# A decoder layer on one core: the last slice of the long convolutions moved from ahead of the delta stage into its first step

## The chip, the cores and the metric

The kernel runs on one core of a Trainium2 chip. The metric is device microseconds (us) from start to end of one execution, as the median of several; less is better. TensorE (PE) does matrix products, with its weight loads shown apart as PEld; VectorE (DVE) and ScalarE (ACT) do elementwise work; GpSimd (POOL) helps; SyncE (SP) issues nearly all DMAs, in the order of its own program.

## The reference

`x` and `ctx` are 8 x 256 x 256, float32. The part that the change touches is the first third:

```python
q, k, v = silu(dwconv(hs @ Wq, conv_q)), ...           # short convolutions, 4 taps
beta = sigmoid(hs @ Wb)
o_d = delta_rule_chunkwise(q, k, v, beta)              # per chunk: T = inv(I - attn); u = T @ v; w = T @ kb; scan over chunks
paths = stack([dwconv(v, fir_s), dwconv(v, fir_m), dwconv(v, fir_l), o_d, v])   # FIRs of 3, 15 and 64 taps
stats = [mean, mean square, mean abs, norm] of every path per head
probs = softmax(gelu([hs, stats] @ gW1 + gb1) @ gW2 + gb2, ...)
o = rmsnorm(sum_p probs_p * paths_p) @ Wo              # then x = layernorm(x + o)
```

Cross attention, a layer norm, and a mixture of 8 experts beside 2 shared ones follow; the change leaves them alone.

## The kernel before

Every engine has its own instruction stream, written out by Python generators; semaphores tie the streams together. `weave(stages, n, before, beside)` runs a software pipeline: in step s it interleaves, round by round (a round ends at each `yield`), stage k on batch s - k for all k, and after them the piece `beside[s]`.

**Projection phase** (`phase_project_invert_and_fir`). It ends with the long convolutions (`pe_fir`): they are products with Hankel matrices of the filters. There are 8 slices (`SLICES`) of 32 channels; slice `sl` reads the matrices in `env.hank[sl % 4]` (four buffers, loaded by SP) and the tokens in `win`. A slice has 4 pairs (`PAIRS`); a pair is 8 products of 128 x 32 weights with 192 columns (16 records in the trace, since each product is recorded twice), into one bank of PSUM: banks 0 to 3 for even slices, 4 to 7 for odd ones. ScalarE copies each pair out (`act_fir`, L685) to `stage[sl // 4]`, a half of the result. Semaphores: `fir_made` counts the pairs that TensorE has made (up to 32), `stage_copied` those that ScalarE has copied. `sp_stage(c)` (L613) writes half c to DRAM (`fir_dram`) in three DMAs of 1024 KB, when `stage_copied` has reached 16 or 32. In the same time VectorE inverts the diagonal blocks of all chunks, 128 of them in each of two groups: `dve_invert(0)`, then `dve_invert(1)` (L633, L636), whose last pieces run beside the delta stage.

**Delta stage** (`phase_delta_and_gate`, a pipeline over the 8 batches). Step s does the inverse of batch s (`pe_invert`, `act_invert`, `dve_invert`), the states of batch s - 1 (`pe_states` ...), the statistics of batch s - 2, the gate of batch s - 3, and the output product of batch s - 4. Rounds of `pe_invert`, which uses banks 0 to 3 only: 0 nothing; 1 turn k (L1053); 2 turn kb = k * beta (L1053; VectorE makes kb at L1167); 3 turn q (L1053); 4 the products kb x k (L1075, `a_made`); 5 the products k x q (L1084, `l_made`); 6 z1 (L1093), from ScalarE's copies at L1143 and L1145; 7 gw1 (L1102); 8 x1 and z2 (L1107, L1111); 9 gw2 (L1119). VectorE ends the step's inverse with L1189. The first instruction of step s + 1 on TensorE waits for that.

SP's order around the change, written out in `sp_first` and the weave: late Hankel matrices, first inverses out, tokens of batches 0 and 1 in (L1023), triangles of batch 0 (L1033, L1034), `sp_stage(0)`, triangles of batch 1, `sp_stage(1)`; then in step 1: the paths of batch 0 in (`sp_states(0)`, L1202 and L1204, which waits for all six writes of `fir_dram`), the tokens of batch 2 (L1023), its triangles, and so on. A DMA that waits holds up all that stand behind it on SP.

Ahead of the delta stage TensorE waits for all 32 pairs copied (`pe.wait_ge(fir.stage_copied, SLICES * PAIRS)`).

Of the kernel before, what the change touches and what calls it, by code (L numbers as in the profile page):

```python
# [15 lines left out]
B, T, D = 8, 256, 256  # L16
# [5 lines left out]
CH = 32  # L22
NCH = P // CH
TAPS = 4
FIRS = (3, 15, 64)
NF = len(FIRS)
# [3 lines left out]
BLK = 64  # L30
# [104 lines left out]
def weave(stages, n, before={}, beside={}):  # L135


    for s in range(n + len(stages) - 1):
        if s in before:
            before[s]()  # L140
        parts = [stage(s - k) for k, stage in enumerate(stages) if 0 <= s - k < n]
        interleave(parts + [beside[s]] if s in beside else parts)


def in_rounds(pieces, rounds):

    for r in range(max(rounds) + 1):
        if r in rounds:
            next(pieces, STOP)
        yield  # L150
# [11 lines left out]
def flat(t):  # L162
    return t.rearrange("p a b -> p (a b)")
# [59 lines left out]
SL = CH  # L223
# [3 lines left out]
HANK_DMAS = len(HANK)  # L227
NG = B * NP * NCH // P
PAIRS = SL // NCH // 2
SLICES = D // SL  # L230
RING = P // SL
# [10 lines left out]
def phase_project_invert_and_fir(pg, a, env):  # L242
    nc, pe, act, dve, pool, sp = pg.nc, pg.pe, pg.act, pg.dve, pg.pool, pg.sp
    V, S, G = nc.vector, nc.scalar, nc.gpsimd
    s = pg.signals("Project", "weights wpad_zero wpad raw_zero sel_zero sel_made filters_turned filters_copied filters_out xT_turned xT_copied raw_made raw_copied beta_made tanh beta first mac silu "
                   "sums_made sums_copied conv_turned sq v_copied ss rn_step tok kT_turned kT_copied a_made diag win_zero win_made fir_made stage_copied small_in tau_log eps_exp small",
                   "x_in rows_in sums_out tok_out diag_out am_in inv_set inv_step turned inv_out")
    with ExitStack() as mem:
# [5 lines left out]
        ps, ident = env.ps, env.ident  # L254
        win = top("win", [P, KT, B * NBLK, P])
# [13 lines left out]
        stage = [views(r, 0, n_stage, "p (f t c) -> p f t c", f=NF, t=BLK) for r in (room0, room1)]  # L269
# [378 lines left out]
        def pe_fir():  # L648
            yield
            yield  # L650
            pe.wait_ge(s.win_zero, 1)
            pe.wait_ge(s.win_made, B)
            pe.wait_ge(s.raw_copied, 3 * B)
            pe.wait_ge(s.sums_copied, B)
            for sl in range(SLICES):
                pe.wait_ge(env.hank_in[sl % RING], 16 * HANK_DMAS * (sl // RING + 1))
                for pair in range(PAIRS):
                    if sl >= 2:
                        pe.wait_ge(s.stage_copied, (sl - 2) * PAIRS + pair + 1)
                    elif sl == 0 and pair == 2:  # L660
                        pe.wait_ge(s.diag, NCH * B)
                    for u in range(2):
                        for q in range(NCH):
                            in_q = sl % RING * SL // NCH + pair * 2 + u
                            m = nc.tensor.matmul(ps[q * CH:(q + 1) * CH, sl % 2 * PAIRS + pair, u * NF * BLK:(u + 1) * NF * BLK],  # L665
                                                 win[:, sl // RING, :, q * CH + in_q],
                                                 env.hank[sl % RING][:, :, :, q * SL // NCH + pair * 2 + u].rearrange("k f s -> k (f s)"),
                                                 start=True, stop=True)
                    m.then_inc(*s.fir_made.up())
                    yield  # L670
                    if sl == 0 and pair == 1:
                        for _ in range(4):
                            yield

        def act_fir():
            for i in range(2):
                act.wait_ge(s.sums_out[i], 16 * B)
                act.wait_ge(s.tok_out[i], 16 * B // 2)
            exponentials = act_small()
            for sl in range(SLICES):  # L680
                next(exponentials, STOP)
                for pair in range(PAIRS):
                    c0 = sl % RING * SL // NCH + pair * 2
                    act.wait_ge(s.fir_made, sl * PAIRS + pair + 1)
                    S.copy(stage[sl // RING].rearrange("p f t c -> p c f t")[:, c0:c0 + 2, :, ::-1],  # L685
                           ps[:, sl % 2 * PAIRS + pair, 0:2 * NF * BLK].rearrange("p (c f t) -> p c f t", c=2, f=NF)
                           ).then_inc(*s.stage_copied.up())

# [57 lines left out]
        pool_win_zero()  # L748
        pool_hank_zero()
        weave([idle, idle, pool_normalise], B)  # L750
    env.sp_stage = sp_stage
    env.sp_inverses, env.sp_late_hank, env.sp_small, env.dve_small, env.projected = sp_inverses, sp_late_hank, sp_small, dve_small, s


# [109 lines left out]
def phase_delta_and_gate(pg, a, env):  # L864
    nc, pe, act, dve, pool, sp = pg.nc, pg.pe, pg.act, pg.dve, pg.pool, pg.sp
    V, S, G = nc.vector, nc.scalar, nc.gpsimd
# [7 lines left out]
    with ExitStack() as mem:  # L874
        def sb(n, shape, dt=F32):
            return mem.enter_context(nc.sbuf_tensor(n, shape, dt))
        ps, ident = env.ps, env.ident
# [21 lines left out]
        uT, u, oT = early("p (t c n) -> p t c n", n_x, 3, c=KT, t=TT)  # L899
# [28 lines left out]
        fir, FIR_OUT = env.projected, 16 * KT * NF  # L928
        GATE_IN, SMALL = 16 * 8, 8
        dve.wait_ge(fir.fir_made, (RING + 1) * PAIRS)  # L930
        pe.wait_ge(fir.stage_copied, SLICES * PAIRS)

        def pool_clear():
            pool.wait_ge(fir.fir_made, (RING + 1) * PAIRS)
# [64 lines left out]
        def dve_scale():  # L999
            dve.wait_ge(s.gate_in, GATE_IN)  # L1000
            V.tensor_scalar(flat(wo[:]), flat(wo[:]), nw[:, 0:1], None, ALU.mult).then_inc(*s.param.up())
            dve.wait_ge(fir.small, SMALL)

        def pe_await():
            pe.wait_ge(s.gate_in, GATE_IN)
# [157 lines left out]
        def dve_invert(b):  # L1163
            i, uses = b % 2, b // 2 + 1
            dve.wait_ge(s.tok_in[i], 16 * uses)
            dve.wait_ge(s.w_made, b - 1)
            V.tensor_tensor(heads(kb[i][:]), heads(tok[i][:, :, 1, :]), beta_of(b), ALU.mult).then_inc(*s.kb.up())  # L1167
            for _ in range(4):
                yield
            dve.wait_ge(s.u1_made, b - 1)  # L1170
            if b == 0:
                dve.wait_ge(fir.fir_made, SLICES * PAIRS)
            V.tensor_tensor(heads(vb[i][:]), heads(tok[i][:, :, 2, :]), beta_of(b), ALU.mult).then_inc(*s.vb.up())
            yield
            dve.wait_ge(s.l_made, b + 1)
            for h in range(HL):
                V.tensor_tensor(by_head(lT[i][:])[:, h], ps[:, 1 + h, :].rearrange("p (q j) -> p q j", j=P),
                                env.causal[:].unsqueeze(1).broadcast_to([P, NP // HL, P]), ALU.mult).then_inc(*s.lT.up())
            yield
            yield  # L1180
            dve.wait_ge(s.gw1_made, b + 1)
            for lo in LOW:
                V.tensor_copy(g0[i][lo:lo + CH, :, lo + CH:lo + 2 * CH],
                              ps[lo:lo + CH, 1, 0:NP * CH].rearrange("p (n j) -> p n j", j=CH)).then_inc(*s.gw.up())
            yield
            yield
            dve.wait_ge(s.gw2_made, b + 1)
            for h, bank in enumerate((3, 0)):
                V.tensor_copy(by_head(g0[i][:])[HS[0], h, :, HS[1]],  # L1189
                              ps[HS[0], bank, 0:NP // HL * DH].rearrange("p (q j) -> p q j", j=DH)).then_inc(*s.gw.up())  # L1190
            yield
# [560 lines left out]
        def rounds(of):  # L1752

            for r in range(max(of) + 1):
                for piece, b in of.get(r, ()):
                    piece(b)
                yield

        C, K, X, Q = pe_context, pe_keys_values, pe_turn_first, pe_first_query
        pe_beside = {9: rounds({3: ((C, 0), (C, 1)), 5: ((K, 0),)}),  # L1760
                     10: rounds({0: ((C, 2), (X, 0)), 1: ((K, 1),), 2: ((C, 3),), 3: ((C, 4),), 4: ((K, 2),), 5: ((K, 3), (C, 5))}),
                     11: rounds({0: ((K, 4),), 1: ((Q, 0),), 2: ((C, 6),), 3: ((K, 5), (C, 7)), 4: ((X, 1), (K, 6)), 5: ((Q, 1),), 6: ((K, 7),)})}
        C, K, X, Q = act_context, act_keys, act_turn_first, act_first_query
        act_beside = {9: rounds({3: ((C, 0), (C, 1)), 5: ((K, 0),)}),
                      10: rounds({0: ((C, 2), (X, 0)), 1: ((K, 1),), 2: ((C, 3),), 4: ((K, 2), (C, 4)), 5: ((K, 3), (C, 5))}),
                      11: rounds({0: ((K, 4),), 1: ((Q, 0),), 2: ((C, 6),), 3: ((K, 5), (C, 7)), 4: ((X, 1), (K, 6)), 5: ((Q, 1),), 6: ((K, 7),)})}
        v, Q = dve_values, dve_first_query
# [10 lines left out]
        sp_first()  # L1778
        weave([sp_invert, sp_states, sp_statistics, sp_gate, sp_project_out], B, {2: sp_rest, 3: sp_cross, 4: sp_filling},
              sp_beside)  # L1780
        weave([pe_invert, pe_states, idle, pe_gate, pe_project_out], B, {3: pe_await, 4: pe_await_scaled}, pe_beside)
        weave([act_invert, act_states, act_statistics, act_gate, act_project_out], B, {}, act_beside)
        weave([dve_invert, dve_states, dve_statistics, dve_gate, dve_project_out], B, {3: dve_scale}, dve_beside)
        pool_clear()
        weave([idle, idle, pool_statistics, pool_gate, pool_project_out], B,
              {9: lambda: pool_by_strip(pg, env, s.cross_in, s.pads, s.by_strip)})
# [1193 lines left out]
```

## Time and profile before

| | |
|---|---|
| median of 3 runs | 940.58 us (933.84, 940.95, 940.58) |
| the profiled execution: its own time | 944.34 us |
| its span, first to last instruction | 942.5 us |
| mean granted TensorE clock | 0.934 of full speed |
| busy share of the span: PE, PEld, DVE, ACT, POOL | 88%, 65%, 63%, 48%, 37% |
| L665, products of the long convolutions (512 records) | 44.2 us busy |

The clock has two levels in the trace, 1.00 (2.4 GHz) and 0.50 (1.2 GHz). Times in rows are us from the span's start. Line numbers of rows are those of the kernel before; in the order of the changed kernel the same lines stand 7 to 15 further down (L665 is L672, L685 is L693, L1053 is L1068).

### The profile page before, as it was taken

What the parts mean: (1) busy time and instruction counts of PE and PEld (TensorE: products, weight loads), DVE (VectorE), ACT (ScalarE), POOL (GpSimd) and SP (SyncE); (2) the same over time, 40 slices, a digit from 0 to 9 for tenths busy, and PEclk for the clock granted to TensorE, in tenths of its full rate; (3) what the DMA queues carried; (4) which work ended last, traced back from release to release, by engine and by line L of the source; (5) the groups of instructions that cost most, each with busy time, mean ns of one, the idle gap of its engine ahead of it and who ended that gap; (6) DMA issues with size and microseconds to landing.
All of it is one profiled execution on the core that took longest, in us unless ns stands there. A gap on an engine that the chain in (4) does not pass through costs nothing.

```text
span 942.5 us, 17146 instructions
## 1 busy us (share of the span) xinstructions
PE 826.7 (88%) x6187; PEld 615.5 (65%) x6187; DVE 592.9 (63%) x1431; ACT 448.9 (48%) x831; POOL 351.4 (37%) x321
## 2 busy tenths in 40 slices
PE   6888879779988988898578898899979999999895
PEld 5676657667766766677345555556866777777784
DVE  4799979664888888877546677763542333333256
ACT  5677747454656564453045665665412322322221
POOL 9421210011546555733202246335531342222684
PEclk9899979886999999799679999999998999999998
DMA  5679849987949875546644455308012222221411
GB/s 174 198 230 292 260 123 252 342 195 175 263 163 259 231 204 155 174 157 208 223 135 166 160 188 179 127 24 268 24 54 78 69 57 68 62 64 45 154 65 67
DMA packets 160722, 149.18 MB, mean 158 GB/s; under 512 B 92288, under 2 KB 129216, under 8 KB 159360
## 3 DMA queue, kind: packets, MB, share of 16 engines
q1 hardware_dynamic: 157232, 138.72, 50.1%
q0 software_dynamic: 3408, 9.38, 2.7%
q8 instruction: 51, 0.84, 0.4%
q14 instruction: 31, 0.25, 0.1%
HBM read 86.90 MB, written 61.03 MB: 157 GB/s over the span
## 4 chain that ended last, share of the span: by engine, by line
PE 54%; DVE 12%; ACT 12%; POOL 8%; DMA 6%; issue 5%; SPq 1%; POOLq 0%; DVEq 0%; ACTq 0%
PE ps L2730 10%; PE ps L2745 5%; PE ps L665 4%; PE ps L2594 3%; DMA queries<-q_pad 2%; DVE big L1449 2%; POOL hank L344 2%; POOL kept L2877 2%; PE ps L1397 2%; PE ps L2103 2%; PE ps L422 2%; PE ps L2216 2%; PE ps L1552 2%; PE ps L1405 2%; POOL hTlo L2664 1%
## 5 line engine op out<-in xcount | busy, mean ns | idle before, releaser
L2730 PE MATMUL ps<-wr,xbT 128*128 x312 | 101.5, 468 | 1.8 <-ACT xbT L2766 1.8
L2153 DVE TENSOR_REDUCE cmx<-ps 128x4 f32<-128x1024 f32 x64 | 77.4, 1219 | 38.0 <-PE ps L2103 36.3
L2192 ACT ACTIVATE cross_room<-ps 128x1024 f32<-128x1024 f32 x64 | 65.5, 1024 | 51.5 <-PE ps L2116 50.9
L2819 POOL DMA_INDIRECT y_dram<-yb,dest_row x39 | 37.5, 961 | 133.1 <-DVE dest_row L2795 128.6
L1365 POOL TENSOR_TENSOR st<-st,exponent 128x20 f32<-128x20 f32 x16 | 56.5, 3533 | 67.7 <-DVE st L1340 66.0
L2730 PEld LDWEIGHTS ps<-wr,xbT 128*128 128x128 f32 x312 | 59.9, 193 | 30.5 <-issue 4.2
L549 DVE SCALAR_TENSOR_TENSOR room<-room 128x256 f32<-128x256 f32 x144 | 58.3, 478 | 11.7 <-ACT room L498 11.7
L2804 DVE TENSOR_TENSOR cross_room<-cross_room,ps 128x352 f32<-128x352 f32 x39 | 20.3, 521 | 61.3 <-PE ps L2730 61.3
L2774 ACT ACTIVATE cross_room<-ps 128x352 f32<-128x352 f32 x39 | 18.1, 465 | 74.4 <-PE ps L2730 74.4
L2810 DVE TENSOR_SCALAR yb<-ps,weight 128x256 f32<-128x256 f32 x39 | 18.9, 484 | 50.8 <-PE ps L2745 50.8
L422 PE MATMUL ps<-room,weights 128*128 128x256 f32 x192 | 46.6, 394 | 3.6 <-DMA room<-in_conv_v 2.9
L665 PE MATMUL ps<-hank,win 128*32 128x192 f32 x512 | 44.2, 513 | 5.0 <-DVE room L583 2.6
L1340 DVE TENSOR_REDUCE st<-paths 128x20 f32<-128x1280 f32 x32 | 47.2, 1479 | 0.2
L422 PEld LDWEIGHTS ps<-room,weights 128*128 128x128 f32 x192 | 37.0, 199 | 9.3 <-DMA room<-in_conv_v 3.3
L665 PEld LDWEIGHTS ps<-hank,win 128*32 128x32 f32 x512 | 32.9, 149 | 15.4 <-issue 4.5
L2664 POOL TENSOR_TENSOR hTlo<-cross_room,hThi 128x512 fp32r<-128x512 f32 (+1 forms) x24 | 31.2, 1300 | 31.3 <-ACT hThi L2623 29.8
L2594 PE MATMUL ps<-x2Thi,whi 128*128 128x512 f32 (+1 forms) x96 | 39.2, 409 | 0.6 <-issue 0.6
L2103 PE MATMUL ps<-keys,queries 49*128 49x256 f32 x224 | 30.0, 347 | 11.1 <-DMA queries<-q_pad 5.5
L2636 DVE TENSOR_TENSOR cross_room<-cross_room,ps 128x512 f32<-128x512 f32 (+1 forms) x24 | 16.4, 685 | 36.2 <-PE ps L2594 15.1
L2176 PE MATMUL ps<-cross_room 128*32 128x256 f32 x512 | 35.9, 400 | 3.0 <-ACT cross_room L2192 2.5
L2594 PE MATMUL ps<-x2Tlo,whi 128*128 128x512 f32 (+1 forms) x96 | 38.5, 401 | 0.0
L2623 ACT CAST hThi<-cross_room 128x512 fp32r<-128x512 f32 (+1 forms) x24 | 14.9, 620 | 48.8 <-DVE cross_room L2636 48.8
(355 smaller groups left out, 2192.1 us busy)
## 6 DMA issues: line engine op xcount, KB each, us to landing
xs_dram<-staged SPq DMA_DIRECT2D x17, 1040.0 KB, 6.6
room<-in_gW SPq DMA_DIRECT2D x8, 1280.0 KB, 8.2
tok_dram<-room SPq DMA_DIRECT2D x8, 768.0 KB, 5.9
fir_dram<-room SPq DMA_DIRECT2D x6, 1024.0 KB, 7.3
paths<-fir_dram SPq DMA_DIRECT2D x48, 128.0 KB, 3.5
keys<-k_pad SPq DMA_DIRECT2D x28, 196.0 KB
queries<-q_pad SPq DMA_DIRECT2D x28, 196.0 KB
xb<-xs_dram SPq DMA_DIRECT2D x39, 130.0 KB, 2.3
```

What stands on the lines that cost most here:

```text
L422: m = nc.tensor.matmul(ps[:, 1 + j, c * T:(c + 1) * T], W[j][:, k, c * P:(c + 1) * P], xT[:, k, :], start=(k == 0), stop=(k == KT - 1))
L549: V.scalar_tensor_tensor(out=conv[:, j, c, :], in0=raw[:, j, c, tap:tap + T], scalar=taps[:, j, c, tap:tap + 1], in1=conv[:, j, c, :], op0 ...
L665: m = nc.tensor.matmul(ps[q * CH:(q + 1) * CH, sl % 2 * PAIRS + pair, u * NF * BLK:(u + 1) * NF * BLK], win[:, sl // RING, :, q * CH + in_ ...
L1340: V.tensor_reduce(st[:, t, k], src[:, :, t, :].rearrange("p n (h d) -> p n h d", h=H), AX.X, ALU.add, **kw).then_inc(*s.stat.up())
L1365: G.tensor_tensor(st[:, t, 3].rearrange("p n h -> p (n h)"), st[:, t, 1].rearrange("p n h -> p (n h)"), env.exponent[:, 1, 0:NPATH * H], A ...
L2103: m = nc.tensor.matmul(ps[:, HL * h + c, t * T:(t + 1) * T], strips(qS[home(b)], slot, c)[:, t * P:(t + 1) * P], strips(kS[home(b)], slot, ...
L2153: V.tensor_reduce(mx[:, :, half, :, g].rearrange("p t c -> p c t"), ps[:, pair(h), :].rearrange("p c (t k) -> p c t k", t=TT), AX.X, ALU.m ...
L2192: S.activation(pT[g % 2][:, pair(h)].rearrange("p c k t -> p (c k t)"), ps[:, pair(1 - h), :].rearrange("p c n -> p (c n)"), ACT.Exp, scal ...
L2594: m = nc.tensor.matmul(ps[0:fn, 2 * par + j, :], w[a_][:, j, k, f0:f0 + fn], env.x2T[b_][:, k, tg * TG:(tg + 1) * TG], start=(k, a_, b_) = ...
L2664: G.tensor_tensor(env.hT[tg % 2][1][0:fn, n, :], env.h[par][0:fn, :], env.hT[tg % 2][0][0:fn, n, :], ALU.subtract).then_inc(*pool.tick(s.lo))
L2730: m = nc.tensor.matmul(ps[:, 2 * (j % 2) + half, 0:FF], xbT[j % 2][:, k, :], wr[:, bass.ds(e, 1), k, half, :].rearrange("p e n -> p (e n)" ...
L2745: m = nc.tensor.matmul(ps[:, 5 + j % 2, 0:D], hbT[j % 2][0:fn, n, :], wdr[n][0:fn, bass.ds(e, 1), :].rearrange("p e n -> p (e n)"), start= ...
```

## The change

The last slice (slice 7, pairs 29 to 32) leaves `pe_fir` and `act_fir`. The bodies become generators `pe_slice` and `act_slice`, and slice 7 is given to the delta stage as the piece beside step 0: one pair after each of the rounds 5, 6, 7 and 8, on TensorE and on ScalarE. TensorE enters the delta stage when 28 pairs are copied, and waits for the 32nd at step 1. VectorE waits for only 24 pairs before it multiplies v by beta for batch 0 (L1173), and for the 32nd at step 1.

```diff
-            for sl in range(SLICES):
-                pe.wait_ge(env.hank_in[sl % RING], 16 * HANK_DMAS * (sl // RING + 1))
-                for pair in range(PAIRS):
...
+            for sl in range(SLICES - 1):
+                for pair, _ in enumerate(pe_slice(sl)):
                     yield
...
-            for sl in range(SLICES):
+            for sl in range(SLICES - 1):
                 next(exponentials, STOP)
...
+                for _ in act_slice(sl):
+                    pass
...
-    env.sp_stage = sp_stage
+    env.sp_stage, env.pe_last_slice, env.act_last_slice = sp_stage, pe_slice(SLICES - 1), act_slice(SLICES - 1)
...
-        pe.wait_ge(fir.stage_copied, SLICES * PAIRS)
+        pe.wait_ge(fir.stage_copied, (SLICES - 1) * PAIRS)
...
+        def pe_await_copied():
+            pe.wait_ge(fir.stage_copied, SLICES * PAIRS)
+
+        def dve_await_fir():
+            dve.wait_ge(fir.fir_made, SLICES * PAIRS)
...
-                dve.wait_ge(fir.fir_made, SLICES * PAIRS)
+                dve.wait_ge(fir.fir_made, (RING + 2) * PAIRS)
...
-        pe_beside = {9: rounds({3: ((C, 0), (C, 1)), 5: ((K, 0),)}),
+        pe_beside = {0: in_rounds(env.pe_last_slice, (5, 6, 7, 8)), 9: rounds({3: ((C, 0), (C, 1)), 5: ((K, 0),)}),
...
-        act_beside = {9: rounds({3: ((C, 0), (C, 1)), 5: ((K, 0),)}),
+        act_beside = {0: in_rounds(env.act_last_slice, (5, 6, 7, 8)), 9: rounds({3: ((C, 0), (C, 1)), 5: ((K, 0),)}),
...
-        weave([pe_invert, pe_states, idle, pe_gate, pe_project_out], B, {3: pe_await, 4: pe_await_scaled}, pe_beside)
+        weave([pe_invert, pe_states, idle, pe_gate, pe_project_out], B, {1: pe_await_copied, 3: pe_await, 4: pe_await_scaled}, pe_beside)
...
-        weave([dve_invert, dve_states, dve_statistics, dve_gate, dve_project_out], B, {3: dve_scale}, dve_beside)
+        weave([dve_invert, dve_states, dve_statistics, dve_gate, dve_project_out], B, {1: dve_await_fir, 3: dve_scale}, dve_beside)
```

TensorE, step 0 of the delta stage, from the products k x q on. Before (all pairs of L665 stand ahead of these):

```order
L1084 MATMUL ps<-kept 128x128 x8
L1093 MATMUL ps<-kept 32x32 x16
L1102 MATMUL ps<-kept 32x32 x16
L1107 MATMUL ps<-ident,kept 64x64 x8
L1111 MATMUL ps<-kept 64x64 x8
L1119 MATMUL ps<-kept 64x64 x8
L1053 MATMUL ps<-ident,kept 128x128 x4
```

And in the changed kernel (L1099 is the old L1084, L1108 the old L1093, L1117 the old L1102, L1122 and L1126 the old L1107 and L1111, L1134 the old L1119):

```order
L1099 MATMUL ps<-kept 128x128 x8
L672 MATMUL ps<-hank,win 32x192 x8
L1108 MATMUL ps<-kept 32x32 x16
L672 MATMUL ps<-hank,win 32x192 x8
L1117 MATMUL ps<-kept 32x32 x16
L672 MATMUL ps<-hank,win 32x192 x8
L1122 MATMUL ps<-ident,kept 64x64 x8
L1126 MATMUL ps<-kept 64x64 x8
L672 MATMUL ps<-hank,win 32x192 x8
L1134 MATMUL ps<-kept 64x64 x8
L1068 MATMUL ps<-ident,kept 128x128 x4
```

Four pairs of eight products have moved in between the inverse's five groups of products; the last one stands ahead of the last group.

ScalarE at the same place, from its last copies of the kb x k products to the first copy of step 1. Before:

```order
L1145 ACTIVATE kept<-ps 64x4x64
L1151 COPY kept<-ps 32x256 x2
L1157 COPY kept<-ps 128x256
L1159 COPY kept<-ps 128x256
L1127 COPY kept<-ps 128x512
```

And in the changed kernel, where L693 is the copy of a pair:

```order
L1160 ACTIVATE kept<-ps 64x4x64
L693 COPY room<-ps 128x2x3x64
L1166 COPY kept<-ps 32x256 x2
L693 COPY room<-ps 128x2x3x64 x2
L1172 COPY kept<-ps 128x256
L1174 COPY kept<-ps 128x256
L693 COPY room<-ps 128x2x3x64
L1142 COPY kept<-ps 128x512
```

The fourth copy of a pair, which is the 32nd of all, now comes after the copies of x1 and z2. SP's order is the same in both.

## Rows read from the trace of the kernel before

**Rows 1.** Chain that ended last, in order of time: start, us, what.
```profile
129.82 41.11 PE ps L665 x442
...
170.96 0.84 ACT room L685
...
171.84 0.67 PE ps L1053 x4
...
201.36 0.42 DVE kept L1189
...
201.91 0.63 PE ps L1053 x4
```

**Rows 2.** Timeline, TensorE and VectorE, step 0: start, us, engine, line [idle before].
```profile
169.38 0.68 DVE L1167 TENSOR_TENSOR kept<-delta_room,beta 128x512 f32<-128x512 f32 x1
172.33 0.60 PE L1053 MATMUL ps<-ident,kept 128*128 128x128 f32 x4
173.75 1.14 PE L1075 MATMUL ps<-kept 64*128 64x96 f32 x16 [0.38 <-ACT kept L1131]
177.02 0.69 PE L1093 MATMUL ps<-kept 32*32 32x32 f32 x32 [1.22 <-ACT kept L1145]
178.59 0.69 PE L1102 MATMUL ps<-kept 32*32 32x32 f32 x32 [0.87 <-issue]
180.24 0.80 PE L1107 MATMUL ps<-ident,kept 64*64 64x64 f32 x10 [0.96 <-DVE kept L1183]
181.11 0.74 PE L1111 MATMUL ps<-kept 64*64 64x64 f32 x10
182.41 1.12 PE L1119 MATMUL ps<-kept 64*64 64x64 f32 x16 [0.56 <-ACT kept L1159]
```

**Rows 3.** Timeline, ScalarE: copies of pairs 28 and 32.
```profile
165.19 0.80 ACT L685 COPY room<-ps 128x384 f32<-128x384 f32 x1 [0.59 <-PE ps L665]
...
170.96 0.83 ACT L685 COPY room<-ps 128x384 f32<-128x384 f32 x1 [0.57 <-PE ps L665]
```

**Rows 4.** Timeline, SP's issues: start, us, engine, line.
```profile
178.60 2.67 SPq L613 DMA_DIRECT2D fir_dram<-room  x3
190.14 4.23 SPq L1202 DMA_DIRECT2D paths<-fir_dram  x6
...
195.46 0.55 SPq L1023 DMA_DIRECT2D delta_room<-tok_dram  x1
```

**Rows 5.** DMA to landing, L613 in 170:173, then L1023 in 195:196.
```profile
DMA to landing us min/median/max: 4.4/6.2/8.7
DMA to landing us min/median/max: 5.5/5.5/5.5
```

**Rows 6.** Stretches: us, busy (x records) of PE, PEld, DVE, ACT, POOL, clock, DMA share, GB/s.
```profile
131.00:135.00 4.00, 4.00 (x54) 2.97 (x49) 3.66 (x11) 1.60 (x2) 0.00 (x0) 0.50 0.39 94
137.00:141.00 4.00, 4.00 (x55) 2.57 (x52) 3.69 (x10) 3.99 (x6) 0.00 (x0) 1.00 1.00 248
...
179.50:182.90 3.40, 2.10 (x42) 1.94 (x43) 3.10 (x10) 0.74 (x2) 0.00 (x0) 0.50 1.18 337
...
184.46:189.60 5.14, 5.14 (x31) 4.41 (x31) 0.46 (x1) 2.20 (x5) 0.00 (x0) 0.50 0.74 311
...
206.80:226.50 19.70, 18.02 (x187) 13.72 (x187) 10.93 (x20) 5.78 (x16) 7.07 (x2) 0.50 0.89 229
...
230.70:243.40 12.70, 12.66 (x94) 9.89 (x92) 9.10 (x12) 9.65 (x19) 7.06 (x2) 1.00 0.92 253
```

**Rows 7.** Timeline: the same work of TensorE at the head of steps 1 and 2.
```profile
184.46 1.08 PE L1053 MATMUL ps<-ident,kept 128*128 128x128 f32 x4 [0.93 <-DVE kept L1189]
...
187.38 1.12 PE L1053 MATMUL ps<-ident,kept 128*128 128x128 f32 x4
...
203.49 0.66 PE L1053 MATMUL ps<-ident,kept 128*128 128x128 f32 x4
...
207.02 1.23 PE L1239 MATMUL ps<-kept 128*128 128x128 f32 x4 [2.04 <-ACT kept L1285]
```

More of the change, by code:

```diff
@@ L654, in pe_fir @@
             pe.wait_ge(s.sums_copied, B)
-            for sl in range(SLICES):
-                pe.wait_ge(env.hank_in[sl % RING], 16 * HANK_DMAS * (sl // RING + 1))
-                for pair in range(PAIRS):
[L658 to L669, printed above, removed]
+            for sl in range(SLICES - 1):
+                for pair, _ in enumerate(pe_slice(sl)):
                     yield
@@ L673, in pe_fir, with pe_slice @@
                             yield
+        def pe_slice(sl):
+            pe.wait_ge(env.hank_in[sl % RING], 16 * HANK_DMAS * (sl // RING + 1))
+            for pair in range(PAIRS):
+                if sl >= 2:
+                    pe.wait_ge(s.stage_copied, (sl - 2) * PAIRS + pair + 1)
+                elif sl == 0 and pair == 2:
+                    pe.wait_ge(s.diag, NCH * B)
+                for u in range(2):
+                    for q in range(NCH):
+                        in_q = sl % RING * SL // NCH + pair * 2 + u
+                        m = nc.tensor.matmul(ps[q * CH:(q + 1) * CH, sl % 2 * PAIRS + pair, u * NF * BLK:(u + 1) * NF * BLK],
+                                             win[:, sl // RING, :, q * CH + in_q],
+                                             env.hank[sl % RING][:, :, :, q * SL // NCH + pair * 2 + u].rearrange("k f s -> k (f s)"),
+                                             start=True, stop=True)
+                m.then_inc(*s.fir_made.up())
+                yield
         def act_fir():
@@ L679, in act_fir, with act_slice @@
             exponentials = act_small()
-            for sl in range(SLICES):
+            for sl in range(SLICES - 1):
                 next(exponentials, STOP)
[L682 to L687, printed above, removed]
+                for _ in act_slice(sl):
+                    pass
+        def act_slice(sl):
+            for pair in range(PAIRS):
+                c0 = sl % RING * SL // NCH + pair * 2
+                act.wait_ge(s.fir_made, sl * PAIRS + pair + 1)
+                S.copy(stage[sl // RING].rearrange("p f t c -> p c f t")[:, c0:c0 + 2, :, ::-1],
+                       ps[:, sl % 2 * PAIRS + pair, 0:2 * NF * BLK].rearrange("p (c f t) -> p c f t", c=2, f=NF)
+                       ).then_inc(*s.stage_copied.up())
+                yield
         def small_views(at, count, n):
```

## The prediction

> **What bounds the kernel now.** I read the chain of waits first. Up to 170.93 us it is TensorE's convolution products, then one copy by ScalarE, and from 171.84 on TensorE's step 0 of the delta stage [rows 1]: nothing overlaps between the two phases. Inside step 0 the timeline shows a ping-pong between engines. TensorE stands idle 1.22, 0.87, 0.96 and 0.56 us ahead of z1, gw1, x1 and gw2 [rows 2]: 3.61 us, the holes into which the change puts its four pairs. So on TensorE's path alone the change looks sound. But a convolution has a second customer. The result must go through DRAM before the statistics can read it, and SP issues that in a fixed order. Its timeline is the view to read next: the three writes of the second half start at 178.60, all are landed at 190.14 (SP stood waiting for them with its next issue), then come the loads of batch 0's paths, and behind them, at 195.46, the tokens of batch 2 [rows 4]. Those land 5.5 us later [rows 5], at 201.0. VectorE ends step 1 at 201.78 and TensorE begins step 2 at 201.91 [rows 1]. Step 2 begins by turning the k of these tokens, and VectorE's first work in it is their kb. So at step 2 two chains arrive 0.8 us apart: TensorE's, and SP's. The change helps the first and delays the second.
>
> **When TensorE can start.** VectorE makes batch 0's kb at 169.38, straight after its inversion steps, and is done at 170.06; this does not move. TensorE turns kb at 172.33 now [rows 2]. In the changed kernel it may go at 170.1: gain 2.2 us, not the 6 us of the slice. ScalarE's copy of pair 28 ends at 166.0 [rows 3], so the turning of k is out of the way long before. The looser wait of VectorE (24 pairs in place of 32) frees its v * beta some 0.9 us earlier; that is off the chain, since its next work for step 0 waits for TensorE. The two waits at step 1 are met well before, and cost nothing.
>
> **What the four pairs cost.** From the copy of pair 28 to that of pair 32 it is 5.77 us [rows 3]: 1.44 us a pair. Put into holes of 1.22, 0.87, 0.96 and 0.56 us, each overhangs: 0.22, 0.57, 0.48, 0.88, in all 2.15 us. ScalarE has room: its copies of 0.83 us run while TensorE is at the next group, and ahead of the z copy one may cost 0.1. So step 0 ends at 184.46 - 2.2 + 2.15 = 184.4: a gain of 0.1 us and no more.
>
> The price of a pair does not hang on the granted clock: 4.0 us hold 54 records at 0.50 and 55 at 1.00 [rows 6]. The Trainium skill ("TensorE: Matmul & The Clock Gate", Back-to-back issue gap) has the gap between products as columns over the clock, so that it doubles at 1.2 GHz; by that rule I would estimate the four pairs at 5.8 us more on the slow clock, and the forecast at some 951. The trace does not agree for these products.
>
> **The clock in step 0.** In the new order TensorE has only the turning of k between the end of pair 28, 165.1, and 170.1. It went down to 0.50 at 206.8, when TensorE had stood idle for most of 2.04 us [rows 6, 7], so I expect it to fall in this hole too. Then the turning of kb and the two groups L1075 and L1084 run slowly. The same turning takes 1.08 to 1.12 us at 0.50 and 0.60 to 0.66 at 1.00 [rows 2, 7], 1.7 times as long; so 0.5, and 0.8 for each group of 1.14 [rows 2], 2.1 us at most, and 0 if it doesn't fall. Against that, the dense pairs may bring it back earlier than now, and x1, z2 and gw2, which ran at 0.50 [rows 6], gain up to 1. I take +1.0 us for the time of the last pair.
>
> **When SP can write the second half.** The last pair now follows x1 and z2, which end at 181.85 [rows 2]. New: 181.85 - 2.2 + (0.22 + 0.57 + 0.48) + 1.44 = 182.4, copied at 183.3, with the clock's 1.0 at 184.3 (183.3 to 185.4). SP's issue goes from 178.60 [rows 4] to there: 5.7 us later. Before, it was held by its own queue, not by the copies, which were done at 171.8 [rows 3]; so all of this is new. From this issue to the last landing it took 11.5 us [rows 4], part of it beside the small transfers of batch 1's triangles, which will be gone by then. Of the first half's three writes, the same bytes, the longest took 8.7 us from its own issue [rows 5], and one may stand a good 1 us behind the first: 9.8 is my lower bound. I take 10.6, between 9.8 and 11.5. The paths of batch 0 then start at 194.9 (193.1 to 196.9), 4.8 us later than 190.14, and everything behind them on SP with them.
>
> **Step 2.** The tokens of batch 2 land at 201.0 + 4.8 = 205.8; step 2 begins 4.0 us later than at 201.8 (bounds 2.2 to 6.0). That TensorE ends step 1 earlier is worth nothing now: 184.46 to 189.60 ran at 0.50 with TensorE busy throughout [rows 6], and the head of a step takes 2.92 us at 0.50 (184.46 to 187.38) and 1.58 at 1.00 (201.91 to 203.49) [rows 1, 7], so some 2.4 of those 5.14 us are to be had. They turn into waiting. And that wait of some 6 us costs once more: the clock falls in it, and the head of step 2, at 1.00 before, runs at 0.50, 2.92 - 1.58 = +1.3 us, and what follows waits for it. Sum: +4.0 + 1.3 = +5.3 us.
>
> **Nothing behind absorbs it.** The statistics, VectorE's reduces and the later steps hang on step 2 in turn, and SP's queue, late by the same, keeps its distance to them. The profiled execution, 944.34 us of its own with a span of 942.5, would become 949.6. It lies 3.8 us above the median of the runs, so **the median forecast is 940.6 + 5.3 = 945.9, say 946 us**. The bounds of this case are 2.2 + 0 and 6.0 + 1.3: 942.8 to 947.9.
>
> **Rivals.**
> 1. *The clock comes back in step 2.* Now 206.80 to 226.50 runs at 0.50 [rows 6]. In step 1 the same kind of work, without a break from 184.46, had the clock back after 5.14 us. A late step 2 on a slow clock gives such an unbroken stretch, as ScalarE's square hides behind slower products. Step 1 took 17.4 us (184.46 to 201.91), 5.1 of them at 0.50; step 2 24.6 (201.91 to 226.5), 19.7 of them at 0.50; of the 7.2 us between them I count 4 as clock, the rest as VectorE's reduces. Sum +5.3 - 4 = +1.3: 941.9 us. Against it: those 19.7 us were busy for 18.02 without its return [rows 6].
> 2. *TensorE's path decides, and SP's not.* If the tokens of batch 2 came in time (a faster landing, an order on SP that I misread), the change keeps 0.1 us of step 0, 1 us of its faster end and 2.4 us in step 1: -3.5, 937.1 us. Against it: 0.8 us of slack stand against 5.7 us of delay at SP.
> 3. *Slower by over 1%: the slow clock outlasts step 2.* The stretch behind 230.70, 12.70 us at 1.00 with TensorE busy 12.66 [rows 6], would take up to 1.8 times as long at 0.50, as the head of a step does [rows 7]. If the shift makes the clock miss its return there, some 8 of these up to 10 us come on top: +13, 953.9 us. It decides when the gate's first products in step 3, which are this stretch, are broken up by waits for weights or statistics.
> 4. *It does nothing on the path.* The order shows the pairs inside step 0, so this is small: 940.6.
>
> **Chances.** My case 0.55; rival 1 0.20; rival 2 0.12; rival 3 0.08; rival 4 0.05. The runs before alone lie 7 us apart (933.84 to 940.95), so 1%, 9.4 us, is about what a measurement of this kernel tells from no change. Faster by over 1% (under 931.2) needs rival 2 and a lucky median: 0.04. Slower by over 1% (over 950): rival 3, and my case with its bounds and an unlucky median: 0.16. Within: 0.80. The range takes in rivals 1 and 2 and half of rival 3: 936 to 952, which also gives the median its share of the spread.
>
> **What would show it.** In the profile after: step 0's kb turned at about 170.1, its last VectorE copy at 184 to 186; SP's L613 of the second half (L622 there) issued at 183 to 185.5 and now released by ScalarE's copy; paths of batch 0 issued at 193 to 197; TensorE's first product of step 2 at 204 to 208, released by the DMA of the tokens and not by VectorE, with 4 us or more of idle before it; clock at 0.50 at that point. If step 2 starts at 202 or earlier, the argument on SP is wrong. If the clock at 210 to 226 is 1.00, rival 1 holds.

## The result, and the profile after

The changed kernel takes 946.65 us, median of 20 runs (939.63 to 954.43), against 940.73 (933.63 to 945.47, 20 runs) of the kernel before beside it: ratio 1.0061 [1.0039, 1.0084], slower by some 6 us. Ratios leave out the runs more than 1.5% above the fastest of their kernel, and in the table below they differ by up to 0.5% from the quotient of the medians beside them. The profiled execution took 945.25 us (span 943.5), hardly more than the 944.34 of before, but it did so at a mean granted clock of 0.945 against 0.934; what that hides is told below.

The chain of waits of the changed kernel, start and length in us. It answers to [rows 1].

```profile
150.70 17.09 DMA delta_room<-tok_dram
...
167.93 2.79 PE ps L1068 x12
170.73 1.96 PE ps L1090 x16
...
180.71 1.62 PE ps L672 x14
...
182.35 0.82 ACT room L693
...
183.19 0.34 SPq L613
...
184.05 10.13 DMA fir_dram<-room
...
194.19 0.37 SPq L1217
...
200.50 4.97 DMA delta_room<-tok_dram
...
205.52 1.11 PE ps L1068 x4
```

Before, the chain went from the convolutions straight into TensorE's step 0, and step 2 began when VectorE had ended step 1. Now it leaves TensorE at the last pair and runs ScalarE's copy (L693), SP's write of the second half (L613), its landing, SP's loads of the paths (L1217), the tokens of batch 2, and only then the first product of step 2. That is the path that the prediction named, link by link. SP's own timeline, for [rows 4]:

```profile
183.19 1.76 SPq L613 DMA_DIRECT2D fir_dram<-room  x3
194.19 5.52 SPq L1217 DMA_DIRECT2D paths<-fir_dram  x6
...
200.50 0.55 SPq L1038 DMA_DIRECT2D delta_room<-tok_dram  x1
```

TensorE's timeline, for [rows 2, 7]; the bracket is the idle time ahead and what ended it:

```profile
167.93 1.09 PE L1068 MATMUL ps<-ident,delta_room 128*128 128x128 f32 x4 [4.18 <-DMA delta_room<-tok_dram]
168.81 1.06 PE L1068 MATMUL ps<-ident,kept 128*128 128x128 f32 x4
170.66 2.03 PE L1090 MATMUL ps<-kept 64*128 64x96 f32 x16
173.85 1.62 PE L672 MATMUL ps<-hank,win 128*32 128x192 f32 x16
...
183.81 0.63 PE L1068 MATMUL ps<-ident,kept 128*128 128x128 f32 x4 [0.94 <-DVE kept L1204]
205.52 1.11 PE L1068 MATMUL ps<-ident,delta_room 128*128 128x128 f32 x4 [7.11 <-DMA delta_room<-tok_dram]
208.47 1.12 PE L1068 MATMUL ps<-ident,kept 128*128 128x128 f32 x4
```

And stretches: length, busy us of PE, PEld, DVE, ACT and POOL with records, granted clock, DMA share, GB/s.

```profile
168.00:173.60 5.60, 5.60 (x42) 5.25 (x44) 2.67 (x6) 2.58 (x6) 0.00 (x0) 0.53 0.85 291
173.60:184.00 10.40, 9.46 (x184) 5.59 (x183) 7.09 (x19) 5.42 (x12) 1.19 (x5) 1.00 0.61 196
184.00:191.50 7.50, 7.38 (x79) 5.69 (x78) 1.54 (x5) 4.97 (x13) 0.00 (x0) 1.00 1.02 418
191.50:194.17 2.67, 2.67 (x52) 1.88 (x52) 2.13 (x6) 1.10 (x3) 0.00 (x0) 1.00 0.03 9
199.20:205.50 6.30, 0.00 (x0) 0.00 (x0) 0.00 (x0) 0.00 (x0) 0.00 (x0) 0.61 0.86 222
205.50:211.00 5.50, 5.35 (x30) 4.28 (x30) 2.09 (x2) 3.37 (x4) 0.00 (x0) 0.52 1.00 241
214.60:221.00 6.40, 4.93 (x29) 3.60 (x30) 4.96 (x7) 1.48 (x5) 5.27 (x2) 0.50 0.95 215
221.00:230.00 9.00, 8.00 (x160) 6.10 (x161) 5.20 (x17) 4.19 (x10) 0.00 (x0) 1.00 0.78 205
```

The two executions are 1.4 us apart already ahead of the change, so I count from a common mark, ScalarE's start on the copy of pair 28 (165.19 before [rows 3], 163.79 after). Six marks carry the comparison:

| us after the mark | before | after | shift |
|---|---|---|---|
| first turning of step 1 | 19.27 | 20.02 | +0.75 |
| SP issues the write of the second half | 13.41 | 19.40 | +6.0 |
| paths of batch 0 issued | 24.95 | 30.40 | +5.45 |
| tokens of batch 2 issued | 30.27 | 36.71 | +6.4 |
| first turning of step 2 | 36.72 | 41.73 | +5.0 |
| ScalarE's square of batch 0 in step 2 | 38.70 | 45.08 | +6.4 |

Behind the square something is given back. I call the stretch from it to the first product of the gate (L1385, L1400 after) the body of step 2. It took 22.56 us before and 18.97 after, since the clock was back at 221.0, and before only behind 226.5 [rows 6]. By the third gate (112.3 us after the mark before, 113.4 after) 5.2 of the 6.4 us are given back. That is rival 1, in this one execution, and the likely reason why its own time is only 0.9 us above before.

### The profile page after: what moved, and what is told of

Read it like the earlier page. It is cut to its first block, busy times and chain, and to the rows that moved or that the text cites. A ratio compares the mean times of both kernels' runs of the same rounds, so it can differ in the third digit from the quotient of the medians.

```text
span 943.5 us, 17146 instructions
## 1 busy us (share of the span) xinstructions
PE 819.6 (87%) x6187; PEld 604.5 (64%) x6187; DVE 593.8 (63%) x1431; ACT 448.5 (48%) x831; POOL 350.9 (37%) x321
## 4 chain that ended last, share of the span: by engine, by line
PE 49%; DVE 15%; ACT 11%; DMA 10%; POOL 8%; issue 5%; SPq 2%; POOLq 0%; DVEq 0%; ACTq 0%
PE ps L2745 10%; PE ps L2760 5%; PE ps L2609 3%; PE ps L1412 3%; DMA queries<-q_pad 3%; DVE big L1464 2%; DMA delta_room<-tok_dram 2%; POOL hank L344 2%; POOL kept L2892 2%; PE ps L2118 2%; PE ps L422 2%; PE ps L2231 2%; PE ps L1567 2%; PE ps L1420 2%; POOL hTlo L2679 1%
## 5 line engine op out<-in xcount | busy, mean ns | idle before, releaser
L549 DVE SCALAR_TENSOR_TENSOR room<-room 128x256 f32<-128x256 f32 x144 | 58.3, 478 | 11.5 <-ACT room L498 11.5
L672 PEld LDWEIGHTS ps<-hank,win 128*32 128x32 f32 x512 | 28.8, 154 | 18.7 <-issue 6.1
L2609 PE MATMUL ps<-x2Thi,whi 128*128 128x512 f32 (+1 forms) x96 | 38.8, 404 | 0.6 <-issue 0.6
L2793 ACT COPY hbT<-ps 128x384 f32<-128x384 f32 x39 | 18.7, 479 | 40.9 <-PE ps L2753 40.9
```

Source lines behind the costliest of these rows:

```text
L549: V.scalar_tensor_tensor(out=conv[:, j, c, :], in0=raw[:, j, c, tap:tap + T], scalar=taps[:, j, c, tap:tap + 1], in1=conv[:, j, c, :], op0 ...
L2609: m = nc.tensor.matmul(ps[0:fn, 2 * par + j, :], w[a_][:, j, k, f0:f0 + fn], env.x2T[b_][:, k, tg * TG:(tg + 1) * TG], start=(k, a_, b_) = ...
```

## Experiments

e1 to e4, e5 to e8 and e9 to e12 ran on one chip each, beside runs of the kernel before on the same chip. "Clock" is the median over the runs of the mean granted clock, with that of before behind the stroke. "Square" is the start of the square after the mark (38.70 before), "body" the body of step 2, both from the one profile of each kernel. A ratio and the quotient of its medians can disagree (e5: 1.0030 and 1.0068; e7: 0.9948 and 0.9988; e4: 0.9895 and 0.9946), so a gain or loss under some 0.5% that only one of the two shows is not settled.

| kernel | ratio to before | medians, us | clock | square | body |
|---|---|---|---|---|---|
| e1_tokens_first | 0.9996 [0.9967, 1.0025] | 946.09 / 946.85 | 0.945 / 0.939 | 39.8 | 19.06 |
| e2_before_tokens_first | 0.9997 [0.9969, 1.0025] | 946.76 / 946.85 | 0.939 / 0.939 | 40.4 | 22.56 |
| e3_before_late_write | 0.9998 [0.9966, 1.0030] | 945.75 / 946.85 | 0.943 / 0.939 | 41.5 | 19.27 |
| e4_one_pair_inside | 0.9895 [0.985, 0.994] | 941.70 / 946.85 | 0.944 / 0.939 | 40.2 | 18.35 |
| e5_later_write | 1.0030 [0.9997, 1.0063] | 951.69 / 945.24 | 0.940 / 0.940 | 48.8 | 19.01 |
| e6_change_again | 1.0086 [1.0043, 1.0130] | 951.14 / 945.24 | 0.937 / 0.940 | 44.8 | 22.55 |
| e7_one_pair_again | 0.9948 [0.9912, 0.9984] | 944.11 / 945.24 | 0.943 / 0.940 | 40.3 | 18.34 |
| e8_one_pair_tokens_first | 0.9951 [0.9920, 0.9981] | 941.52 / 945.24 | 0.944 / 0.940 | 37.1 | 22.55 |
| e9_before_filled | 1.0009 [0.9990, 1.0028] | 939.75 / 939.96 | 0.944 / 0.942 | 38.8 | 22.56 |
| e10_one_pair_first_filled | 0.9997 [0.9974, 1.0021] | 939.72 / 939.96 | 0.944 / 0.942 | 37.5 | 22.56 |
| e11_change_filled | 1.0058 [1.0035, 1.0080] | 944.32 / 939.96 | 0.948 / 0.942 | 45.0 | 21.42 |
| e12_tokens_first_again | 1.0017 [0.9996, 1.0037] | 939.93 / 939.96 | 0.947 / 0.942 | 39.6 | 18.99 |

**e1: the tokens of batch 2 ahead of the paths.** The changed kernel, with one load moved on SP:

```diff
 def sp_invert(b):
+            if b == 1:
+                sp_tokens(2)
             for _ in range(4):
                 yield
             if 0 < b < B - 1:
-                sp_tokens(b + 1)
+                if b > 1:
+                    sp_tokens(b + 1)
```

> The changed kernel, with one thing moved on SP: in step 1 the load of the tokens of batch 2 is issued ahead of the loads of batch 0's paths, so it no longer stands behind the late write of the convolutions' second half. Theory (the write delayed on SP is the cost): the tokens land before 195, step 2 starts straight after VectorE's last copy of step 1 (near 199 in place of 205.5), its square starts when the paths are there, near 204 in place of 208.9, and nearly all of the loss is gone: 0.999 to 1.002 times the time of the kernel before (940 to 943 us). Rival (the cost is on TensorE: four pairs between the groups of step 0, or the clock there): nothing changes, 1.005 to 1.007.

By the medians the loss is gone. TensorE and ScalarE at the head of step 2:

```profile
202.31 0.63 PE L1071 MATMUL ps<-ident,delta_room 128*128 128x128 f32 x4 [0.93 <-DVE kept L1207]
...
206.16 2.34 ACT L1350 ACTIVATE sqs<-paths 128x2560 f32<-128x2560 f32 x1 [1.76 <-DMA paths<-tok_dram]
...
209.29 1.22 PE L1257 MATMUL ps<-kept 128*128 128x128 f32 x4 [3.91 <-ACT kept L1303]
```

Step 2 is released by VectorE again, at full clock (0.63 us a turning); what is late now are the paths, for which the square waits 1.76 us, and TensorE then waits 3.91 us for ScalarE's next copy (2.04 before [rows 7]). So the load behind the write was the loss in the medians, as the theory of SP's order has it; the four pairs on TensorE are all still there. The changed kernel itself did not run on this chip, so it is compared through the kernel before. What is left of the loss at an equal clock is told further down.

**e2: the same move in the kernel before**, as its control.

> The kernel before, with the same move on SP as the control: tokens of batch 2 ahead of batch 0's paths. Theory: in the kernel before these tokens arrive 0.8 us before TensorE is ready, so at most noise: 0.999 to 1.001. If this move by itself gains as much as it does in the changed kernel (0.5%), the first experiment says nothing of the delayed write.

It measures 0.9997: the move by itself is worth nothing. So what e1 gains over the change is no gain of that order in itself. Its profile also shows how far one profile can be trusted: VectorE releases step 2 as before, and yet the square comes at 40.4, not at 38.7, as TensorE's head of step 2 ran partly at the slow clock. Shifts of the square under 2 us are no more than such a difference.

**e3: the delay alone.** In the kernel before SP waits for the last products of the inverse in step 0 (gw2):

```diff
                 sp_triangles(b)
+                if b == 1:
+                    sp.wait_ge(s.gw2_made, 1)
                 env.sp_stage(b)
```

> The kernel before, all products where they were; SP alone waits for gw2's products of step 0 (near 183.5) before it writes the convolutions' second half, which it issued at 178.6: the delay of the change without the change. Theory: tokens of batch 2 land near 205 to 206, TensorE is idle for 4 us ahead of step 2, the clock falls: 1.004 to 1.007 times the time before (945 to 947 us). Rival (the cost is TensorE's): the kernel before, 0.999 to 1.001.

The write was issued at 181.56, 4.9 us later than in the profile of e2 (176.65), which shares its chip. Step 2 did wait:

```profile
201.02 1.11 PE L1055 MATMUL ps<-ident,delta_room 128*128 128x128 f32 x4 [2.16 <-DMA delta_room<-tok_dram]
```

But the square moved by only 2.8 us, since the write, alone on the queues, had landed 9.0 us after its issue (190.52) instead of 11.5, and in the body the clock was back early, 19.27 us for 22.56. The runs show no loss at all, against my expectation. Against e2, its neighbour on the chip, the square is only 1.0 us later, so this delay was too small to decide anything by its time.

**e4 and e7: one pair inside.** Three pairs return to the convolutions, the last goes behind the k x q products:

```diff
+            for _ in range(3):
+                next(env.pe_last_slice)
+                yield
...
-        pe_beside = {0: in_rounds(env.pe_last_slice, (5, 6, 7, 8)), ...
+        pe_beside = {0: in_rounds(env.pe_last_slice, (5,)), ...
```

> The change with one pair in place of four: three pairs of the last slice stay ahead of the delta stage, in the hole in which TensorE waits for the first tokens (4.2 us), the fourth stands between the products k x q and z1. The last copy is done near 176, before SP's queue comes to the write at 178.6. Theory: no delay on SP, loss gone; on TensorE some 2 us earlier, of which the tokens of batch 2 let through 0.8: 0.997 to 1.000 (938 to 941 us). Rival (any pair inside step 0 costs): 1.001 to 1.003.

e4 gave 0.9895, from six runs, which I had repeated:

> The form with one pair inside step 0 again, as its first 6 runs gave 0.9895, more than the sum allows (its profile has step 2's tokens landing at the time of the kernel before). Theory: 0.997 to 1.000. If it is 0.990 again, the gain has a source outside SP's queue, and the clock of the later steps is where to look.

0.9948 [0.9912, 0.9984], again under the forecast, but 0.9988 by the medians. In its profile the last pair is copied at 172.26 and SP writes at its own turn, 176.10: nothing is held. The square is 1.6 us later than before all the same, and the gain sits in the body (18.34).

```profile
199.55 1.12 PE L1074 MATMUL ps<-ident,delta_room 128*128 128x128 f32 x4 [4.12 <-DMA delta_room<-tok_dram]
```

Here TensorE is early and the tokens are not late: they come 36.9 us after the mark, where step 2 began at 36.72 before. The time won in steps 0 and 1 has turned into 4.12 us of waiting, the clock is down after it, and the square stands 3.35 us behind the first turning, as in the change. So the slow head comes with the wait, whether SP's delay or TensorE's own gain has made the wait.

**e5: the write later still.** As e3, with the wait on `s.u`, which ScalarE raises with its first copy of u in step 1.

> A second dose of the delay without the change: the kernel before, with SP waiting for ScalarE's first copy of u in step 1 (near 189.8) ahead of the second half's write, 11 us later than it issued it. In the first dose the write, alone on the DMA queues, landed in 9.0 us in place of 11.5, so only some 2.3 us of 4.9 came through to step 2. Theory: here 11 - 2.5 = 8.5 us come through, less 0.8 of slack, plus 1.3 for a slow head of step 2: +9 us, 1.007 to 1.012 times the time before. Rival (SP's write does not matter, the cost of the change is TensorE's): 0.998 to 1.002.

```profile
189.45 1.77 SPq L613 DMA_DIRECT2D fir_dram<-room  x3
200.00 4.07 SPq L1204 DMA_DIRECT2D paths<-fir_dram  x6
...
205.05 0.55 SPq L1025 DMA_DIRECT2D delta_room<-tok_dram  x1
```

```profile
210.49 1.11 PE L1055 MATMUL ps<-ident,delta_room 128*128 128x128 f32 x4 [9.61 <-DMA delta_room<-tok_dram]
```

The write is issued 11.0 us later after the mark than before, and nearly all of that reaches step 2: the square is 10.1 us later. 3.6 us come back in the body. The ratio, 1.0030, is under what I expected, and its interval takes in 1; the medians are 6.4 us apart. A cost is likely by this run and not shown, and it is less than the delay's length.

**e6: the change once more**, beside e5, e7 and e8.

> The changed kernel itself, beside the others on their chip. If the loss is of the change and not of one chip: 1.004 to 1.008 again.

1.0086, just above the forecast. Its profile has the other outcome in the body; one stretch, from the first product of step 2:

```profile
204.40:230.30 25.90, 23.30 (x216) 17.96 (x216) 13.55 (x22) 9.92 (x21) 7.07 (x2) 0.50 0.86 218
```

The clock stays at 0.50 throughout, and the body takes 22.55 us as before. So the same kernel shows either outcome, and what stands when the clock does not come back is the whole delay of the square, 6.1 us here (forecast 5.3).

**e8: one pair inside and the tokens first.**

> One pair inside step 0, and on SP the tokens of batch 2 ahead of batch 0's paths. Theory: TensorE's 2 us of step 0 and the 2.4 us of a faster step 1 can reach step 2 now, until the paths stop ScalarE's square: these land near 199, where TensorE would want them near 200. 0.995 to 0.998 times the time before (936 to 939 us). Rival (SP's order without effect): the same as the run with one pair and the old order.

0.9951. Here the gain is of another kind: the square is 1.6 us earlier than before, and the body is the long one.

**e9 to e11: filling TensorE's holes.** To see whether the idle time at the head of step 2 is what takes the clock down, TensorE multiplies the identity by itself into a bank that is free there; these products are extra work, and nothing reads them. Four of them ahead of the turning of q in the kernel before (e9) and in e8 (e10); 14 ahead of step 2 and 3 ahead of that turning in the change (e11).

```diff
+        def pe_fill():
+            for n in (4,):
+                for _ in range(n):
+                    nc.tensor.matmul(ps[:, 7, 0:P], ident[:], ident[:], start=True, stop=True)
+                yield
...
-        pe_beside = {9: ...
+        pe_beside = {2: in_rounds(pe_fill(), (2,)), 9: ...
```

> The kernel before with four products of the identity by itself (1.7 us at the full clock, into bank 7, read by nobody) ahead of the turning of q in step 2, where TensorE stands idle for 2.0 us beside ScalarE's square. Theory (in the body of step 2 the clock decides, and it fell in that hole): the granted clock stays at 1.00 or is back early in step 2, and the square-to-gate stretch of batch 0 takes 19 us in place of 22.6: 0.995 to 0.998. Rival (VectorE's reduces set that stretch, the clock is incidental): 0.999 to 1.001.

```profile
198.80:205.60 6.80, 5.65 (x58) 4.69 (x58) 4.30 (x4) 4.81 (x7) 0.89 (x1) 1.00 0.74 235
205.60:208.00 2.40, 0.10 (x4) 0.01 (x2) 2.34 (x5) 1.83 (x6) 2.40 (x1) 0.83 1.07 234
208.00:223.30 15.30, 14.74 (x166) 10.93 (x166) 6.68 (x15) 3.29 (x8) 3.78 (x2) 0.50 0.88 209
```

The four products took 1.06 us and left 1.15 us of the hole open. The clock held through it, and fell in the next hole, 2.29 us in which TensorE waits for a copy of VectorE's (L1313) that stands behind its reduces. From there on all was as before: 1.0009, where I had expected 0.995 to 0.998.

> One pair inside step 0, tokens of batch 2 first on SP, and the same four filling products in step 2. Its unfilled form had the square at the earliest point of all runs but a slow clock after it. Theory: both gains add, some 1.6 + 3.5 us: 0.990 to 0.995. Rival: as unfilled, 0.995.

0.9997, missed as well, and with the same long body. Its square is 1.2 us early, as that of e8 was 1.6, and here the runs show nothing of it; e8's 0.9951 is the less to be leaned on.

> The changed kernel with 14 filling products (5.9 us) in TensorE's 7 us of waiting for the tokens of batch 2, and three beside ScalarE's square. SP's delay stays, the clock's part of the loss should go: the head of step 2 runs at 1.00 (1.6 us in place of 2.9) and the body has no slow stretch. Theory (of the loss of some 5.5 us, 4 are the wait and the rest, more in executions with a slow body, is clock): 1.001 to 1.004. Rival (all of it is the wait): 1.006 to 1.008.

```profile
194.55 3.39 PE L1777 MATMUL ps<-ident 128*128 128x128 f32 x28
...
201.91 1.11 PE L1068 MATMUL ps<-ident,delta_room 128*128 128x128 f32 x4 [3.98 <-DMA delta_room<-tok_dram]
```

14 products took 3.39 us, 0.24 each, and left 3.98 us of the wait open: the clock fell, and the head was slow as in the change. Behind the head it was back (0.99 from 207 to 214), and fell again in a wait of 2.3 us for VectorE: hence a body of 21.42, between the other two values. The kernel did not do what it was made for, and says nothing on the price of the clock. Its 1.0058, above the forecast, stands beside the change's own 1.0061.

**e12: e1 again**, beside these.

> The changed kernel with the tokens of batch 2 ahead of batch 0's paths, again, on a second chip or at another time: 0.997 to 1.001, against 1.0086 and 1.0061 of the changed kernel in its own order.

1.0017 [0.9996, 1.0037], just above the forecast; step 2 released by VectorE, the square waiting 1.64 us for the paths. With e1 (0.9996) against the change's 1.0061 and 1.0086 this is the clearest pair of the study. The two forms never ran side by side; the nearest to that is e11, the change with its fillers, on this chip: 944.32 against 939.93 us.

**What the clock of the runs adds.** Each run lists its mean granted clock, and within a kernel the time goes with it: the 35 runs of before beside e5 to e8 have a correlation of -0.74, from 948.28 us at 0.932 to 932.06 at 0.955 (-0.71 over the 22 that the ratios use). I put a straight line through the runs of each kernel that the ratios use, and read both at 0.942. Distance to before there: e6, the change, +5.5 us (± 1.3); e5 +5.5 (± 1.1); e3 +2.2 (± 1.7); e1 +2.5 (± 2.1) and e12 +3.6 (± 2.5); e2 +0.2 (± 1.9); e7 0.0 (± 1.9); e8 -0.1 (± 1.3); e4 -1.5 (± 2.1); e9 +1.3 (± 1.5); e10 +0.5 (± 1.5); e11 +5.8 (± 3.9). With every run in, e5 and e6 come to +4.8 and +4.6. So the delays do cost: 5.5 us for the 10.1 by which e5's square is late, as much for the 6.1 of e6, some 2 for the 2.8 of e3. They are partly hidden in the medians by a higher clock. e1 and e12 still lose 2 to 4 us, by their late paths as I read it, which no run shows apart, and win them back with the clock (0.945 and 0.947, against 0.937 of e6). At an equal clock the move of the one load thus takes away about half of the loss and not all of it; and what e7 and e8 gain goes with the clock. A caution: the clock is in part the kernel's own doing, so this splits a difference, it does not correct it.

## Why the prediction was right

**The bound and the path.** Right: TensorE's gain is swallowed, and SP's queue sets step 2. The profile of the change shows the path, and e1 and e12 show that the loss goes, by the medians, when the load is taken out from behind the write; e3 and e5 show that holding the write by itself, with no pair moved, brings the same wait (TensorE idle 2.16 and 9.61 us for the same load). Rival 2, TensorE's path deciding, is out. Rival 4, nothing, too. Rival 3 was not seen: in e6, the profile with the longest slow stretch, the clock is back at some 234, 4 us behind the gate's first product (230.31), just as before (226.45 and 230.7).

**When TensorE can start.** kb was turned 5.0 us after the mark (168.81), forecast 4.9. The reason was only half right. I had VectorE's kb as the limit; the tokens of batch 0, issued at 150.70 and landed 17.1 us later, stopped TensorE before that for 4.18 us. VectorE waited 0.39 us for the same tokens before it could make kb, so the two limits lie some 0.4 us apart here, and the number held by luck. In e1 it was the other way round: there TensorE waited 0.89 us for kb.

**What the pairs cost.** Forecast 1.44 us each less the holes, step 0 ending 0.1 us earlier at a steady clock. Measured: 1.55 on the chain (1.61 or 1.62 in the timeline, in every profile), and step 0 ends 0.75 later. The slow clock accounts for most: at 0.53 until 173.6 the products kb x k took 2.03 us for 1.14 [rows 2]. The +1.0 that I had put down for it was right in kind and size. The pairs of the change ran at 1.00 throughout. Only in e1 was one partly at 0.50:

```profile
176.82 1.62 PE L672 MATMUL ps<-hank,win 128*32 128x192 f32 x16
...
177.00:177.50 0.50, 0.50 (x8) 0.27 (x8) 0.50 (x1) 0.15 (x1) 0.00 (x0) 0.50 0.87 344
177.50:178.00 0.50, 0.50 (x12) 0.24 (x4) 0.50 (x2) 0.00 (x0) 0.00 (x0) 0.97 1.19 475
```

The first 0.7 of its 1.62 us were at 0.50, and it took no longer than its neighbours at 1.00 (1.61 and 1.62). That speaks for the prediction's reading. By the Trainium skill's rule ("TensorE: Matmul & The Clock Gate", Back-to-back issue gap) products at 0.50 take twice as long; this one pair does not agree with it, and no profile has a whole pair at 0.50 in this place.

**SP's write.** It stands at L613 in the changed kernel too, not at the L622 of the prediction. The copy ended 19.4 us after the mark, forecast 19.1. Issue to paths 11.0 us, forecast 10.6 (9.8 to 11.5). The DMA engines moved 418 GB/s from 184.00 to 191.50, and 9 GB/s in the 2.67 us after that; the landing waited for an end that moves almost nothing. The Trainium skill ("DMA: Bandwidth & Descriptors", Anatomy of one DMA — SWDGE (gpsimd) path) puts most of a DMA's fixed cost of about 2 us into the confirmation that the last byte has landed, longest for HBM. That section is on DMAs issued by GpSimd, and these are SP's; the 2.67 us here are longer than its whole fixed cost, and in e3 the same tail was 0.70 us, so the traces agree that there is such a tail, and not that it is constant. My lower bound of 9.8 was too high (9.0 in e3).

**Step 2.** Forecast +4.0 and +1.3 for its head at the slow clock. Measured +5.0 and +1.37 (the square 3.35 us behind the first turning, 1.98 before); idle 7.1 us, forecast "some 6". The 1.0 on the first is SP's: tokens issued 6.4 us later for 4.8 forecast, of which 0.6 are the later write and its slower landing, and the rest the loads of the paths, whose issue took 5.52 us on SP for 4.23 before [rows 4]. Landing took 4.97 for 5.5, and gave 0.5 back.

**Nothing behind absorbs it.** This is the weakest step. The square is 6.4 us late in one profile and 6.1 in the other, the runs lose 5.9: right in sum. But the body of step 2 has two values in nearly all profiles, about 19 and 22.6 us, and so rival 1, at 0.20, is no rival but an outcome that the same kernel has on some executions: in the profile of the change it came, in that of e6 not. My price for it was 4 us; the body gave 3.6, and 5.2 by the third gate. How many of the change's 20 runs had the short body is not known. That the median of 946.65 lies within 1 us of the 946 forecast is therefore partly luck: the square came 1.1 us later than the forecast's +5.3, and some executions gave time back that the forecast let stand.

**What decides the body stays open.** Profiles with the short body: the change, e1, e3, e4, e5, e7, e12. With the long one: before, e2, e6, e8, e9, e10; e11 lies between. Those with a wait for a load near the head of step 2 mostly have the short one, but e6 waits 6.30 us and has the long one. A short body is also not always time won. From the square to the third gate before takes 73.6 us; the change, e3, e4, e5 and e7 are 5.0 to 5.9 us quicker, e1 and e12 only 2.1 and 1.7, e11 1.1, and the others are within 0.5 us of before. e9 and e10 show that filling the first hole of the long ones is not enough; a kernel that fills the second as well was not tried. That the slow head cost the runs its 1.4 us is likewise read from profiles alone, since e11 failed to take it away.

**A version that beats both?** One pair inside (e4, e7) is faster by 0.5 to 1% in the ratios of two comparisons, by 0.5 and 0.1% in their medians. I would call it a candidate and not a finding, since its gain goes with the clock: at equal clock e7 equals the kernel before.

## What to carry to other kernels

Before work is moved into another engine's idle time, follow its result to the second customer: here four pairs in 3.6 us of holes held back a 3 MB write, and a load queued behind it that has nothing to do with the pairs. Where a DMA queue is served in order, ask for each instruction that may wait who stands behind it; one load moved ahead (e1, e12) undid a loss of 6 us in the medians, about half of it at an equal clock. And time that one engine wins only helps if the next load is there: with one pair inside (e7) it became 4.12 us of waiting. And compare the granted clock of two executions before their times: own times 0.9 us apart hid medians 5.9 us apart.

## What the runs showed of the hardware

- A load of tokens (one DMA) landed 4.97 us after its issue at 200.50, and 17.09 us after it at 150.70, when other transfers stood ahead of it.
- 3 MB in three writes landed 9.0, 10.6 and 11.0 us after the first issue (e3, e5, the change), and 11.5 to 12.1 with other transfers between them (12.1 in e10); the time from the last data to the landing was between 0.70 and 2.67 us.
- A pair of the long convolutions took 1.61 or 1.62 us between other groups in every profile that has it there, also in e1, where the clock was at 0.50 for its first 0.7 us; in an unbroken row it took 1.44.
- TensorE's clock fell in waits of 2.29 us (e9) and 7.11 us (the change), and came back in the midst of step 2 in one execution of the changed kernel and not in another, 3.6 us apart in the body.
